# A decoder layer in one kernel: the orders of the first products, of both layer norm borders and of the cross-attention loop rewritten

## What is computed

```python
q_c  = rms_norm(x @ wq_down.T, q_norm_w);  kv_c = rms_norm(x @ wkv_down.T, kv_norm_w)
k_rope = rope(x @ wk_rope.T);  q_pe = rope(q_c @ wq_rope.T)
out = softmax(mask(cat(q_nope, q_pe) @ cat(k_nope, k_rope).T * scale)) @ v
x = layernorm(x + out @ wo.T)
q = x @ Wq.T;  k, v = split(ctx @ Wkv_expand.T)
x = layernorm(x + softmax(mask(q @ k.T / sqrt(32))) @ v @ Wout.T)
x = layernorm(x + shared_experts(x) + top2_of_16_experts(x))
```

## Time and profile before

| | us |
|---|---|
| median of 3 runs | 901.39 |
| lowest, highest | 900.47, 902.63 |
| profiled execution | 902.72 |
| its span | 900.9 |
| PE busy in it | 838.2 |
| DVE, ACT, POOL busy | 528.1, 474.8, 240.8 |

### The profile page before, as it was taken

How to read it: one execution, slowest core, us unless ns; L and a number is a source line. 1 busy time by engine, 2 the same in 40 slices (tenths; PEclk the granted TensorE clock), 3 DMA queues, 4 the chain that set the end, 5 groups by cost and what they waited for, 6 DMA issues and landing times.

```text
span 900.9 us, 13299 instructions
## 1 busy us (share of the span) xinstructions
PE 838.2 (93%) x4302; PEld 710.2 (79%) x4302; DVE 528.1 (59%) x979; ACT 474.8 (53%) x1225; POOL 240.8 (27%) x278
## 2 busy tenths in 40 slices
PE   6978999999999987889998789999999999999997
PEld 5766888788788775777776678888888988889896
DVE  3553753654664557666767755636465665656467
ACT  5514752743753554676576651525473745637150
POOL 0222230132132021455455100431232332321420
PEclk9989999999999998999999999999999999999999
DMA  8022315133322400321222020543464564653432
GB/s 324 1 78 63 123 43 157 65 99 98 123 85 55 146 21 21 84 49 38 55 52 67 2 71 24 183 166 119 146 206 164 187 199 153 198 166 131 137 94 82
DMA packets 39486, 96.33 MB, mean 107 GB/s; under 512 B 15824, under 2 KB 21840, under 8 KB 37808
## 3 DMA queue, kind: packets, MB, share of 16 engines
q1 hardware_dynamic: 28384, 57.95, 20.6%
q0 software_dynamic: 11056, 37.79, 12.9%
HBM read 71.59 MB, written 20.97 MB: 103 GB/s over the span
## 4 chain that ended last, share of the span: by engine, by line
PE 62%; issue 15%; DVE 8%; ACT 7%; POOL 4%; SPq 1%; DMA 1%; POOLq 0%; ACTq 0%; DVEq 0%
PE ps L1490 50%; ACT Pt L829 3%; PE ps L1505 3%; PE ps L1830 2%; POOL Pt L593 2%; PE ps L1820 1%; PE ps L1550 1%; PE ps L1640 1%; DVE negmax L1101 1%; SPq L514 1%; DVE acc L1117 1%; PE ps L1711 1%; PE ps L1832 1%; DVE kb L1218 1%; DVE stats L1123 1%
## 5 line engine op out<-in xcount | busy, mean ns | idle before, releaser
L593 POOL TENSOR_TENSOR Pt<-Pt,rowinv 112x448 f32<-112x448 f32 x64 | 59.9, 936 | 226.6 <-DVE rowinv L1108 226.2
L829 ACT ACTIVATE Pt<-ps,negmax 112x112 f32<-112x112 f32 x256 | 87.2, 356 | 49.1 <-DVE negmax L1101 49.0
L1490 PE MATMUL ps<-x2T_hi,ws_hi 128*128 128x448 f32 x256 | 96.0, 375 | 4.3 <-DVE x2T_lo L1030 4.3
L1490 PE MATMUL ps<-x2T_lo,ws_hi 128*128 128x448 f32 x256 | 94.2, 368 | 0.0
L1490 PE MATMUL ps<-x2T_hi,ws_lo 128*128 128x448 f32 x256 | 94.1, 368 | 0.0
L1490 PE MATMUL ps<-w_hi,h_hi 128*128 128x512 f32 x224 | 89.9, 401 | 0.0
L957 ACT ACTIVATE hf<-ps,b 128x448 f32<-128x448 f32 x64 | 40.6, 635 | 92.3 <-PE ps L1490 72.9
L1490 PE MATMUL ps<-w_hi,h_lo 128*128 128x512 f32 x224 | 88.5, 395 | 0.0
L1490 PE MATMUL ps<-w_lo,h_hi 128*128 128x512 f32 x224 | 88.4, 395 | 0.0
L1030 DVE TENSOR_TENSOR h_lo<-hf,h_hi 128x448 fp32r<-128x448 f32 x64 | 39.9, 623 | 48.7 <-ACT h_hi L958 47.9
L1374 DVE TENSOR_TENSOR acc<-ps,acc 128x512 f32<-128x512 f32 x56 | 38.6, 689 | 44.4 <-PE ps L1490 35.4
(11 more groups left out here) (282 smaller groups left out, 2248.6 us busy)
## 6 DMA issues: line engine op xcount, KB each, us to landing
stage<-in_wf SPq DMA_DIRECT2D x30, 513.0 KB
rows_in<-in_zeros SPq DMA_DIRECT2D x30, 256.0 KB, 4.0
xs<-rows_in POOLq DMA_DIRECT2D x29, 256.0 KB, 4.3
rows_out<-yb POOLq DMA_DIRECT2D x29, 256.0 KB
stage<-in_wa SPq DMA_DIRECT2D x4, 1408.0 KB, 6.6
stage<-in_wb SPq DMA_DIRECT2D x4, 1280.0 KB, 5.6
qr<-ro_hi SPq DMA_DIRECT2D x64, 56.0 KB, 2.0
qr<-ro_lo SPq DMA_DIRECT2D x64, 56.0 KB, 2.0
```

Source lines behind the costliest of these rows:

```text
L593: nc.gpsimd.tensor_tensor(p, p, rowinv[0:S, b % 2, :].unsqueeze(2).broadcast_to([S, GH, S]), ALU.mult).then_inc(norm_done, 1)
L829: last = nc.scalar.activation(Pt[0:S, b % 2, h * S:(h + 1) * S], ps[0:S, b % 2, h * S:(h + 1) * S], ACT.Exp, bias=negmax[0:S, b % 2, h:h + 1],
L1490: ins = mm(dst, w, x, start=start and i == 0, stop=stop and i == len(ops) - 1, skip_group_check=not (start and stop))
```

## The change

Nothing is added to or taken from the arithmetic. Orders are rewritten and some work changes its engine.

- **Start.** ACT issues a Sqrt of one element before its first copy. PE starts the first k slice with the high by high terms of four batches once two `hi` pieces are there, and the `lo` terms follow.
- **First part of self attention.** The second half of the latents, the rotary keys and the value splits become items (LAT, RMS, NAT, VAL, KR) with their own orders on PE, ACT and DVE. A 0, A 1, E 0 and O 0 use banks 2, 3, 0 and 1. The three `wa_lo` pieces move from POOL to DVE. Rotary keys are added, rounded and lowered on POOL. SP waits for all four key products before it packs.
- **First border.** The four memsets of `kb` move to POOL (behind LK, N 7 and L). V 0 leaves the last self attention part for the first cross part. ROW 6 goes to DVE in both borders. W 5 stands before U 0 and U 1. After W 6 come Q 0, U 4, U 5 and only then S 0. F 2 and F 3 go to the very end of POOL's cross order. S 4, Z 1 and T 3 join the first part.
- **Cross loop.** Its body runs from step 5 to 12 rather than from 4 to 11. LK and L go one step later, X on POOL too (from behind N 5 to behind N 6 and Z 3). Q 0 goes behind T 5. W 1 goes from step 8's fill to its end (on DVE to step 9), W 5 and W 6 behind S 4 of the next group.
- **Second border.** W 1 goes behind T 6 and Z 5, W 3 behind T 7, FF 0 before W 5 and W 6, and ACT takes U 4 to 6 before FF 1.

```diff
-ROWS_ON_DVE = [2, 3]
+ROWS_ON_DVE = [2, 3, 6]
-ATT_PRE = [("E", 0), ("O", 0), ("A", 0), ("R", 0), ("E", 1), ("A", 1), ("A", 2), ("O", 1), ("Q", 0, 0),
-           ("R", 1), ("Q", 1, 0), ("Q", 2, 0), ("Q", 3, 0), ("Q", 0, 1), ("G", 0), ("SB", 0), ("Q", 1, 1)]
+_lat0, _lat1 = [("LAT", b) for b in range(HB)], [("LAT", b) for b in range(HB, B)]
+_kvn = [("VAL", b) for b in range(HB, B)]
+_q = [("Q", 1, 0), ("Q", 2, 0), ("Q", 3, 0), ("Q", 0, 1), ("G", 0), ("SB", 0), ("Q", 1, 1)]
+ATT_PRE = _lat0 + [("KR", 0), ("A", 0), ("A", 1), ("E", 0), ("O", 0)] + _lat1 + [
+    ("KR", 1), ("A", 2), ("E", 1), ("O", 1), ("Q", 0, 0)] + _q
+ATT_PRE_ACT = _lat0 + [("RMS", 1), ("A", 0), ("A", 1)] + _kvn + _lat1 + [
+    ("R", 0), ("A", 2), ("Q", 0, 0), ("Q", 1, 0), ("Q", 2, 0), ("Q", 3, 0), ("R", 1)] + _q[3:]
+ATT_PRE_DVE = _lat0 + [("RMS", 1), ("KR", 0), ("NAT", 1), ("A", 0), ("A", 1), ("E", 0), ("O", 0)] + _lat1 + [
+    ("KR", 1)] + _kvn + [("A", 2), ("E", 1), ("O", 1), ("Q", 0, 0)] + _q
+PRE_BANK = {("A", 0): 2, ("A", 1): 3, ("E", 0): 0, ("O", 0): 1}
...
-    ("Z", 6), ("T", 7), ("U1", 0), ("U1", 1), ("W", 5), ("Z", 7), ("U1", 2), ("U1", 3), ("V", 0), ("W", 6)]
+    ("Z", 6), ("T", 7), ("W", 5), ("U1", 0), ("U1", 1), ("Z", 7), ("U1", 2), ("U1", 3), ("W", 6)]
...
+ATT_LAST_POOL = weave(range(8), _pool, fill={5: [("CX",)], 6: [("LK",), ("KB", 0)],
+                                             7: [("KB", 1), ("L",), ("KB", 2), ("KB", 3)]})
...
-X_PRE_POOL = [("F", 0), ("N", 0), ("F", 1), ("N", 1), ("F", 2), ("N", 2), ("F", 3), ("N", 3)]
+X_PRE_PE = [("Q", 0), ("U1", 4), ("U1", 5), ("S", 0), ("V", 0), ("K", 1), ("S", 1), ("U1", 6), ("T", 0), ("S", 2),
+            ("V", 1), ("Q", 1), ("T", 1), ("S", 3), ("Z", 0), ("T", 2), ("S", 4), ("Z", 1), ("T", 3)]
+X_PRE_POOL = [("F", 0), ("N", 0), ("N", 1), ("F", 1), ("N", 2), ("N", 3), ("N", 4), ("Z", 1)]
-X_PE = weave(range(4, 12), [("S", 0), "fill", ("Z", 3), ("T", 1), "late"], wrap=True, fill={
-    5: [(NEXT, "K", 0)], 6: [(NEXT, "Q", 0)], 7: [(NEXT, "V", 0)], 8: [(NEXT, "K", 1), ("W", 1)],
-    9: [("W", 2), (NEXT, "Q", 1)], 10: [("W", 3), ("W", 4)], 11: [(NEXT, "V", 1)]},
-    late={7: [("W", 0)], 11: [("W", 5), ("W", 6)]})
+X_PE = weave(range(5, 13), [("S", 0), "fill", ("Z", 3), ("T", 1), "late"], wrap=True, fill={
+    5: [(NEXT, "K", 0)], 7: [(NEXT, "V", 0)], 8: [(NEXT, "K", 1)], 9: [("W", 2), (NEXT, "Q", 1)],
+    10: [("W", 3), ("W", 4)], 11: [(NEXT, "V", 1)], 12: [("W", 5), ("W", 6)]},
+    late={6: [(NEXT, "Q", 0)], 7: [("W", 0)], 8: [("W", 1)]})
+X_DVE = weave(range(5, 13), [("Z", 4), ("N", 1), ("S", 0), "early", ("T", 2), "fill"], wrap=True, fill={
+    5: [(NEXT, "K", 0)], 6: [(NEXT, "Q", 0)], 7: [(NEXT, "V", 0)], 8: [(NEXT, "K", 1)],
+    9: [("W", 2), (NEXT, "Q", 1)], 10: [("W", 3), ("W", 4)], 11: [(NEXT, "V", 1)], 12: [("W", 5), ("W", 6)]},
+    early={8: [("W", 0)], 9: [("W", 1)]})
-X_POOL = weave(range(4, 12), ["early", ("N", 0), ("Z", 3), "fill"], wrap=True, fill={
-    4: [(NEXT, "L")], 5: [("X",)]}, early={4: [(NEXT, "LK")]})
+X_POOL = weave(range(5, 13), ["early", ("N", 0), ("Z", 3), "fill"], wrap=True, fill={
+    5: [(NEXT, "L")], 6: [("X",)]}, early={5: [(NEXT, "LK")]})
...
+X_LAST_PE = [
+    ("S", 5), ("Z", 2), ("T", 4), ("S", 6), ("Z", 3), ("S", 7), ("W", 0), ("T", 5), ("Z", 4), ("T", 6), ("Z", 5),
+    ("W", 1), ("W", 2), ("Z", 6), ("T", 7), ("W", 3), ("Z", 7), ("U2", 0), ("U2", 1), ("W", 4), ("U2", 2), ("U2", 3),
+    ("FF", 0), ("W", 5), ("W", 6), ("FF", 1), ("U2", 4), ("U2", 5), ("U2", 6), ("FF", 2), ("FF", 3)]
+X_LAST_POOL = [("N", 5), ("X",), ("N", 6), ("Z", 3), ("N", 7), ("Z", 4), ("Z", 5), ("Z", 6), ("Z", 7), ("F", 2),
+               ("F", 3)]
...
+            sp.wait_ge(kr_done, 4)
             pack(0, 0)
...
+            nc.scalar.activation(warm[:, :], one[:, :], ACT.Sqrt)
...
+            for i, (arrived, n) in enumerate(((in_hi, 2), (in_lo, 1), (in_lo, 2))):
+                pe.wait_ge(arrived, n)
+                for b in range(HB):
+                    mm(ps[0:S, b, :], *down_terms(b, 0)[i], start=i == 0, stop=False, skip_group_check=True)
```

More of the change, by code:

```diff
@@ L238, in count, with first_after @@
         return self.per[item[0]] * g + self.rank[item] + 1
+    def first_after(self, places, item):
+        n = places.index(item)
+        return None if n > 1 else [i for m, i in enumerate(self.pre if places is self.body else self.last)
+                                   if m % 2 == n][-1]
     def base(self, g):
@@ L246, in place @@
         n = places.index(item)
-        if n >= 2:
+        if places is self.pre and item in PRE_BANK:
+            return Place(PRE_BANK[item] - 6, number + n, None, None)
+        if n >= 2 and places[n - 2] not in PRE_BANK:
             dg, prev = group_of(places[n - 2])
@@ L258, with turns @@
 Place = namedtuple("Place", "bank number prev prev_count")
-AJ = Jobs(0, ATT_PRE, ATT_PE, ATT_LAST_PE, "AEOQGBWKV")
+AJ = Jobs(0, ATT_PRE, ATT_PE, ATT_LAST_PE, "AEOQGBWK")
 XJ = Jobs(AJ.end, X_PRE_PE, X_PE, X_LAST_PE, "QKVW", X_DONE)
-def turns(fori, jobs, pre, body, last, step, between=None):
+def turns(fori, jobs, pre, body, last, step):
     def run(order, places, g, number):
@@ L773, in _, with squares @@
             copy(maskb[0:S, :], maskf[0:S, :]).then_inc(const_done, 1)
-            for r in range(2):
+            def squares(r):
                 for b in range(HB * r, HB * r + HB):
@@ L891, in att_step @@
                     row(0, j)
-                elif kind == "EXP":
-                    function_ready(ACT.Exp)
                 elif kind == "SQRT":
@@ L934, in x_step @@
                     turned(0, j, x1T_hi)
-                elif kind == "ROOT1":
-                    layernorm_root(0, j)
-                elif kind == "ROW1":
-                    row(0, j)
+                elif kind == "EXP":
+                    function_ready(ACT.Exp)
                 elif kind == "ROOT2":
@@ L1047, in _, with rms @@
             dve.wait_ge(c_ld, 64)
-            for r in range(2):
+            def rms(r):
                 rows = slice(HB * r, HB * r + HB)
@@ L1185, in att_step @@
                     ins.then_inc(a_free[kind], 1)
+                elif kind == "LAT":
+                    dve.wait_ge(tr_hi, j + 1)
+                    cols = slice(j * S, (j + 1) * S)
+                    low(qkT_lo[:, :, cols], ps[:, j, 0:4 * S].rearrange("p (c s) -> p c s", c=4),
+                        qkT_hi[:, :, cols]).then_inc(tr_lo, 1)
+                elif kind == "RMS":
+                    rms(j)
+                elif kind == "NAT":
+                    latents(j)
+                elif kind == "VAL":
+                    values(j)
+                elif kind == "KR":
+                    for s in range(2):
+                        dve.wait_ge(kr_done, 2 * j + s + 1)
+                        ins = nc.vector.tensor_tensor(batches(rope_keys[j][:, s, :]),
+                                                      batches(ps[:, 2 * j + s, 0:HALF]), table(2 + s), ALU.mult)
+                    ins.then_inc(kr_mul, 1)
                 elif kind == "SA":
@@ L1515, in turn_latents, with rope_key @@
                 ins.then_inc(tr_done, 1)
[L1517 to L1521 removed]
+            def rope_key(half):
+                pe.wait_ge(in_lo, 2 * KD + 2)
                 for s in range(2):
                     bank = 2 * half + s
[L1525 removed]
+                    if half:
+                        pe.wait_ge(a_free["A"], AJ.count(("A", s), 0))
+                    else:
+                        pe.wait_ge(tr_lo, s + 1)
                     cols = slice(half * HALF, (half + 1) * HALF)
@@ L1530, in _ @@
                         .then_inc(kr_done, 1)
-                if half == 0:
-                    for b in range(HB, B):
-                        turn_latents(b)
-            pe.wait_ge(tr_lo, B)
             def heads(ap):
```

201 lines of the change are left out of this document (103 added, 98 removed), and 28 rows, old and new, of tables (ATT_LAST_ACT, ATT_LAST_DVE, X_LAST_ACT, X_LAST_DVE).

## The result

The changed kernel takes 929.4 us (median of four runs, 924.5 to 930.0) against 901.3 us before: 1.030 times the time, with an interval of 1.027 to 1.033. The sign was forecast right. The size was not: the forecast was 913 us, and the range ended at 927. Only the third rival (928 us) named a time that near.

What follows compares the result with a forecast made beforehand. PE bounds the kernel, busy 838.2 of 900.9 us. From the profiled 902.7: - 2.0 - 12.7 - 6.0 - 4.5 + 31.5 (loop) + 5 (low clock) = 914.0, forecast 913 as median; range 888 to 927.

Steps and rivals of the forecast that it cites:

- third rival: Chance 0.14: the new waits outside the loop are larger and the loop costs its upper bound; + 27, 928 us.
- Start and first part: Up to S 0: gains of 2.0 us at the start and 12.7 us in the first part of self attention.
- (a): Cross loop: K 0 waits for LK, which now stands behind N 4 and Z 1 on POOL; 4.5 us a run.
- (d): Cross loop: X, later on POOL, holds the key DMAs on SP and so S 0, and W 0; + 6.0 us a run.
- (e): Cross loop: W 1 no longer waits 0.9 us, but Q 1, in the same bank, waits 1.5 us for W 1's add.
- (b): Cross loop: L comes 4.6 us after K 0, with 3.5 of PE work; 1.1 us a run.
- (g): Cross loop: low clock after the long waits, 0.7 us behind K 0 and 1.0 behind S 0; 5 us in all.
- First border: From self to cross attention: four memsets leaving DVE and the new order gain 6.0 us; bounds 3 and 9.
- W 5 and W 6 wait 1.2 to 2.5 and 1.6 us: First border: Z 6's and Z 7's low halves stand later on DVE, so these two products wait that long.
- + 1.0: First border: a gain of 1.0 us in the sum 5.1 + 1.7 - 1.2 + 1.0 - 0.6 = 6.0.
- Second border: From cross attention to the experts: the new order gains 4.5 us; bounds 1.5 and 8.
- by durations it is 34.9 us: Second border: its length in the new order, against 38 us from S 5 to the expert product before.

Runs made afterwards that it cites:

- the kernel with the first part alone: The kernel before with only the start and first part of self attention as in the changed kernel; 885.1 us, 0.981 of the time before.
- the one with the gap: The changed kernel, with POOL starting L and two memsets behind it only once DVE has written rows 2 and 3 of the first norm; 923.7 us.

## Why the prediction was wrong, point by point

**Start and first part: right.** 16.35 us against 14.7, within the bounds. Of the wait forecast at 2.0 us for the values on DVE 0.64 us came: the four splits took 2.6 us together, and not 1.79 each as the one in the earlier trace rows did beside POOL's long items. Self attention gave back 1.2 us, of which 1.09 is a wait right behind S 0 for a query's low half.

**Cross loop: right.** (a) K 0 waits 3.5 to 4.2 us (forecast 4.5). (d) S 0 waits 3.3 to 4.2 and W 0 2.0, together 5.3 to 6.2 a run (6.0). (e) Q 1 waits 0.6 to 1.1 (1.5). (b) hardly shows: 0.2 us once; PE ran at the low clock ahead of it (the first window below). (g) was forecast at 1.7 us a run and is worth 1.7 to 1.8 or a little more. Together 37.9 us against 36.5. All the signs that the prediction named came: 45 us a run, both waits, 0.50 in the clock.

```profile
379.30:382.70 3.40, 3.31 (x12) 2.96 (x12) 0.71 (x2) 0.54 (x1) 0.37 (x2) 0.50 0.00 0
393.10:403.20 10.10, 6.46 (x18) 5.04 (x19) 2.31 (x5) 2.39 (x11) 1.09 (x2) 0.50 0.28 71
```

These windows of the first run lie behind K 0's wait and from W 0's through S 0's.

**First border: here the prediction failed.** It took four memsets off DVE at a gain of 5.1 us, and that gain is there: W 3 waits 0.70 instead of 3.37, and W 4 is done 24.0 us after W 0 starts instead of 29.2. Then it let them run on POOL at no cost, by two-input splits alone. The failing step is "W 5 and W 6 wait 1.2 to 2.5 and 1.6 us". W 6 waits 1.40. W 5 waits 6.58, because VAR's add was held, which I had priced like its median. Against the 1.2 to 2.5 forecast that is 4.1 to 5.4 us of the 10.6, 4.7 in the middle. The low clock behind it makes W 5 itself 4.76 us long instead of 3.03 (1.7 us). A second stretch of 6.8 us at 0.50 lies behind T 0's wait of 2.76, which was forecast at 2.9 without a stretch; it lengthens V 1 and Q 1 by 2.9 us:

```profile
362.30:369.10 6.80, 6.80 (x26) 6.25 (x25) 1.88 (x4) 2.19 (x10) 3.21 (x3) 0.50 0.42 104
```

And Q 0 waits 0.78 for W 6's add, which had no term. Sum 10.1. In the recorded sum the + 1.0 has no row and no working, and the order's share of it (6.0 less the 5.1 of the memsets) did not come either: in the table above the new order is 0.8 us slower than the old one.

The trace of before had the warning. DVE, then POOL, in the kernel before:

```profile
350.13 1.97 DVE L1133 TENSOR_SCALAR rstd<-mv 128x4 f32<-128x4 f32 x1
```

```profile
349.91 0.94 POOL L593 TENSOR_TENSOR Pt<-Pt,rowinv 112x448 f32<-112x448 f32 x1 [5.46 <-DVE rowinv L1108]
350.80 1.28 POOL L601 TENSOR_TENSOR wx_lo<-stage,wx_hi 128x512 fp32r<-128x512 f32 x1
```

1.97 us for an add with a median of 169 ns, to 0.02 us behind L's end. The third rival had this mechanism in words ("VAR, ROOT and ROW on DVE now meet four memsets and L on POOL") and a time of 928, but no price of its own: it was given as bounds. From this row the price could have been worked out. POOL's items from N 7 on are 0.93, 1.6, 1.3 and 3.1 long; the sum is 6.9, and 6.55 was measured.

**Second border: the gain was not there.** 0.6 us against 4.5, under the lower bound. The stall of the earlier trace rows is gone, but PE waits 3.58 before Z 7 (forecast 2.5), 1.62 before FF 0 and 1.73 before U 4, and runs at 0.50 for a stretch after Z 7. FF 0 and FF 1 cover W 5 and W 6 as forecast; what they can't cover is that rows and their splits come from DVE and ACT, whose chain is no shorter. The step that failed is "by durations it is 34.9 us": it counted PE's durations and one wait, where DVE's queue sets the time, as the run with T 7 moved shows. Even the 0.6 us is no gain that can be told: the old order took 416.3 us in the kernel with the first part alone, the new one 417.1 in the changed kernel.

**The sum.** The direction hung on the loop, and that was priced within 4%. The borders' forecast gain of 10.5 us became a loss of 4.0. That the third rival's 928 lies near 929.4 is luck: it took 42 us for the loop with its clock and 15 for all gains, where 37.9 and 11.2 were measured, and the two errors cancel.

## What to carry to other kernels

Before a step is moved to an idle engine, list what the other engines run in that stretch that shares something with it, and look in the trace for the worst case of each of these instructions, not for its median: an add with a median of 169 ns and one value of 1970 is a price tag. Where POOL gets work near a short DVE chain that others wait for, leave a gap in POOL's list, with a wait if there is no other way. When a change mixes moves of single items with a new order, run each without the other: here the new first part and, once repaired, the memsets' move gave all the gain, and the new orders of both borders and the loop none. In a loop with software-made orders, find the items without slack on both sides (here LK to K 0 and X to S 0) and let nothing stand ahead of them, on the queue that raises the semaphore and on the queue that waits for it.

## What the runs showed of the hardware

- In these runs a DVE tensor_scalar on fp32 in SBUF is not served between POOL's instructions. It waited through five in a row (6.55 us), two (2.27 us, and 1.97 in the kernel before), and ran in 0.17 us where POOL was idle. By the Trainium skill (SBUF — State Buffer, Who interferes with whom) the second to come waits until the first has finished its instruction; here it waited until POOL's queue ran dry. The changed kernel, the one with the gap and the kernel before show it.
- The same add with two SBUF inputs was held by a reading POOL instruction and not by the memset after it (0.73 us). Another one, started during a memset (329.79), took 1.71 us, until the L split behind that memset was done. Why it didn't finish in the memset's last 0.4 us stays open; the rule on two SBUF inputs doesn't say it.
- A subtraction with two SBUF inputs was let in between two POOL instructions that read. In the kernel before, POOL's items ran from 41.04 to 43.41 and from 43.37 to 45.81; the `kvN_lo` of the earlier trace rows started at 41.77 and ended at 43.56, right behind the first of them.
- PE's clock was at the 1.2 GHz level (0.50) in stretches that began in or behind waits of 2.04 to 6.58 us in the loop and the borders; three of them lasted 3.4, 6.8 and 10.1 us. Unused products in the waits brought two runs of the loop from 0.84 to 0.96 and the loop 5.5 us forward.
